# What paces GpSimd's gathers in the first layer: landings of earlier gathers instead of TensorE's progress

## The reference

```python
h = relu(layernorm(x))                                   # 6250 x 128
ef = (relu(edge_attr_64 @ We1 + be1) @ We2 + be2) * sigmoid(edge_weight * Wt + bt)
msg = relu(concat([h[src], ef]) @ Wn1 + bn1) @ Wn2 + bn2
x = x + segment_sum(msg, dst) + h                        # first layer
h = relu(layernorm(x))
h2 = h + segment_sum(h[src], dst)
x = x + relu(relu(h2 @ W1 + b1) @ W2 + b2)               # second layer
```

## Time and profile before

| | us |
|---|---|
| median of three runs | 2865.11 |
| lowest and highest run | 2864.87, 2867.78 |
| span of the profiled execution | 3603.9 |
| GpSimd busy in it | 2098.5 |
| TensorE busy in it | 2652.8 |

### The profile page before, as it was taken

How to read it: one execution, slowest core, us unless ns; L and a number is a source line. 1 busy time by engine, 2 the same in 40 slices (tenths; PEclk the granted TensorE clock), 3 DMA queues, 4 the chain that set the end, 5 groups by cost and what they waited for, 6 DMA issues and landing times.

```text
span 3603.9 us, 51709 instructions
## 1 busy us (share of the span) xinstructions
PE 2652.8 (74%) x14584; PEld 1610.3 (45%) x14585; DVE 1962.6 (54%) x4063; ACT 1009.1 (28%) x1000; POOL 2098.5 (58%) x2125
## 2 busy tenths in 40 slices
PE   4687788877877778778877788785645766766766
PEld 3344444444444444444444444343332545544544
DVE  8665566655656566656655566665673333233333
ACT  3233333333333333333333333232231111111112
POOL 6566666666666666666666665555254555555552
PEclk8788888888888888878888888887875777877777
DMA  6444444444433343444344343333122434334332
GB/s 196 113 127 134 127 127 136 125 130 128 126 121 125 123 124 122 123 125 124 120 122 128 120 128 115 120 117 96 32 101 83 132 118 129 122 95 128 101 114 61
DMA packets 229418, 426.82 MB, mean 118 GB/s; under 512 B 82703, under 2 KB 141584, under 8 KB 229072
## 3 DMA queue, kind: packets, MB, share of 16 engines
q0 software_dynamic: 74752, 153.23, 16.3%
q1 hardware_dynamic: 103152, 177.42, 15.0%
q10 hardware_dynamic: 51266, 93.34, 7.4%
HBM read 364.35 MB, written 59.43 MB: 118 GB/s over the span
## 4 chain that ended last, share of the span: by engine, by line
PE 39%; issue 20%; DVE 17%; another core or an unknown queue 12%; DVEq 10%; SPq 1%; DMA 1%; ACT 0%; POOL 0%; ACTq 0%
PE ps L925 9%; PE ps L836 8%; PE ps L795 8%; DVE nodes L1185 5%; PE ps L804 5%; PE ps L815 4%; PE ps L787 3%; DVEq L1119 3%; DVEq L1165 2%; DVE hot L1140 2%; DVE acc L1127 1%; DVE arena L1185 1%; DVEq L1182 1%; PE ps L915 1%
## 5 line engine op out<-in xcount | busy, mean ns | idle before, releaser
L537 POOL DMA_INDIRECT big<-table,idx x2080 | 2032.9, 977 | 1375.8 <-issue 587.6
L836 PE MATMUL ps<-nodes 128*128 128x500 bf16 x1280 | 448.5, 469 | 335.8 <-DVE nodes L1185 180.3
L795 PE MATMUL ps<-arena,we 128*128 128x512 f32 x784 | 511.9, 784 | 29.7 <-issue 12.2
L640 ACT ACTIVATE big<-big 128x1024 f32<-128x1024 f32 x196 | 207.2, 1057 | 1074.3 <-DVE big L1134 917.5
L815 PE MATMUL ps<-hot,big 128*128 128x64 f32 x3136 | 395.9, 275 | 112.8 <-issue 86.0
L1185 DVE TENSOR_SCALAR nodes<-iota_k,win_off,nodes 128x500 bf16<-128x500 f16 x1280 | 453.7, 407 | 0.0
L815 PEld LDWEIGHTS ps<-hot,big 128*128 128x128 f32 x3136 | 381.6, 195 | 107.0 <-issue 104.6
L1182 DVE TENSOR_TENSOR nodes<-iota_b,nodes 128x384 bf16<-128x384 f16 (+1 forms) x492 | 245.4, 499 | 266.8 <-remote 174.8
L1134 DVE TENSOR_TENSOR big<-ps,big 128x1024 f32<-128x1024 f32 x196 | 239.3, 1221 | 244.2 <-issue 242.6
L836 PEld LDWEIGHTS ps<-nodes 128*128 128x128 bf16 x1280 | 106.3, 106 | 573.6 <-DVE nodes L1185 271.1
L630 ACT ACTIVATE arena<-ps,cols 128x1024 f32<-128x1024 f32 x196 | 218.5, 1115 | 418.7 <-PE ps L787 229.2
(11 more groups left out here) (147 smaller groups left out, 2534.2 us busy)
## 6 DMA issues: line engine op xcount, KB each, us to landing
arena<-in_ew SPq DMA_DIRECT2D x196, 512.0 KB
arena<-in_ea SPq DMA_DIRECT2D x196, 256.0 KB
counts_d<-arena ACTq DMA_DIRECT2D x192, 245.0 KB
acc<-counts_d ACTq DMA_DIRECT2D x15, 2940.0 KB
big<-table,idx POOLq DMA_INDIRECT x2080
table<-big SPq DMA_DIRECT2D x7, 672.0 KB, 3.0
idx<-in_src SPq DMA_DIRECT2D x260, 4.0 KB
xs<-in_x SPq DMA_DIRECT2D x7, 448.0 KB, 5.5
```

Of the source, the lines that this page charges most:

```text
L537: pool.indirect_dma_start(to(u, q, t), None, table, bass.IndirectOffsetOnAxis(ap=idx[:, u, at:at + 1], axis=0))\
L795: pe.matmul(p_ef[q], we2[:, :], hid[:, q, :], start=True, stop=True).then_inc(ef_mm, 1)
L836: m = pe.matmul(to, hots[:, t, :], keys[:, t, :], start=False, stop=True, skip_group_check=True)
```

## The change

The semaphore of a block's gathers becomes two, one for its gathers 0 and 2 and one for 1 and 3. In front of every gather after the first 32, GpSimd now waits for the landing of the gather before the last one. The waits for `ef_mm` and `agg_mm` go, in all bodies. The waits for `pre_made` and for the indices stay. TensorE increments `hid_mm`, `ef_mm` and `pre_mm` once a pair, by two, with its last instruction. SyncE and VectorE wait for four semaphores in place of two. `paced_pair` with `apart=True` belongs to a loop that these inputs don't enter.

```diff
-        gathered = [[sem(f"gathered{u}{q}") for q in (0, 1)] for u in range(RING)]
+        gathered = [[[sem(f"landed{u}{q}{h}") for h in (0, 1)] for q in (0, 1)] for u in range(RING)]
...
                     for q in (0, 1):
-                        sp.wait_ge(gathered[u][q], b * (16 * TB))
+                        for h in (0, 1):
+                            sp.wait_ge(gathered[u][q][h], b * (8 * TB))
...
+            def gather_one(table, to, u, q, t, landed):
+                at = q * TB + t
+                pool.indirect_dma_start(
+                    to(u, q, t), None, table,
+                    bass.IndirectOffsetOnAxis(ap=idx[:, u, at:at + 1], axis=0))\
+                    .then_inc(landed, 16)
...
+            def paced_pair(b, u, apart):
+
+                for q in (0, 1):
+                    for t in range(TB):
+                        if t >= 2:
+                            pool.wait_ge(gathered[u][q][t % 2], b * 32 + 16)
+                        elif q:
+                            pool.wait_ge(gathered[u][0][t % 2], b * 32 + 32)
+                        elif u:
+                            pool.wait_ge(gathered[u - 1][1][t % 2], b * 32 + 32)
+                        else:
+                            pool.wait_ge(gathered[RING - 1][1][t % 2], b * 32)
+                        if apart:
+                            pool.sem_inc(pairs_begun, 1)
+                        gather_one(table0, to_rows, u, q, t, gathered[u][q][t % 2])
...
-            def gather_body(b, free=False):
+            def gather_body(b, apart):
                 for u in range(RING):
                     pool.wait_ge(pre_made, b * (2 * RING) + (2 * u + 2 - 2 * RING))
                     pool.wait_ge(idx_loaded[u], b * 16 + 16)
-                    if not free:
-                        pool.wait_ge(ef_mm, b * (2 * RING) + 2 * u)
                     pool.sem_inc(pairs_begun, 1)
-                    gather_block(table0, to_rows, u, 0, gathered)
-                    if not free:
-                        pool.wait_ge(agg_mm, b * RING + (u - 2))
-                    pool.sem_inc(pairs_begun, 1)
-                    gather_block(table0, to_rows, u, 1, gathered)
+                    paced_pair(b, u, apart)
...
-                    pe.matmul(p_hid[q], we1[k, :], ea_s[k, u, :], start=True, stop=True).then_inc(hid_mm, 1)
+                    i = pe.matmul(p_hid[q], we1[k, :], ea_s[k, u, :], start=True, stop=True)
+                i.then_inc(hid_mm, 2)
...
-                    i.then_inc(pre_mm, 1)
+                i.then_inc(pre_mm, 2)
...
                 for q in (0, 1):
-                    dve.wait_ge(gathered[u][q], (s * NBODY + b) * (16 * TB) + 16 * TB)
+                    for h in (0, 1):
+                        dve.wait_ge(gathered[u][q][h], (s * NBODY + b) * (8 * TB) + 8 * TB)
```

More of the change, by code:

```diff
@@ L532, in _ @@
                 pool.tensor_tensor(x_g, x_g, stages[g % 2], ALU.add).then_inc(xh_made, 1)
+            def gather_one(table, to, u, q, t, landed):
[4 more added lines that the diff above has]
+                    .then_inc(landed, 16)
             def gather_block(table, to, u, q, landed):
                 for t in range(TB):
[L536 to L540, removed]
+                    gather_one(table, to, u, q, t, landed[u][q])
             def gather_pair(table, to, u, landed):
@@ L552, in _ @@
             pool.wait_ge(table0_stored, 16 * NG)
+            def paced_pair(b, u, apart):
[12 more added lines that the diff above has]
+                        gather_one(table0, to_rows, u, q, t, gathered[u][q][t % 2])
             for u in range(RING):
                 pool.wait_ge(idx_loaded[u], 16)
-                gather_pair(table0, to_rows, u, gathered)
-            def gather_body(b, free=False):
+                for q in (0, 1):
+                    for t in range(TB):
+                        gather_one(table0, to_rows, u, q, t, gathered[u][q][t % 2])
+            def gather_body(b, apart):
                 for u in range(RING):
@@ L560, in gather_body @@
                     pool.wait_ge(idx_loaded[u], b * 16 + 16)
-                    if not free:
-                        pool.wait_ge(ef_mm, b * (2 * RING) + 2 * u)
                     pool.sem_inc(pairs_begun, 1)
-                    gather_block(table0, to_rows, u, 0, gathered)
-                    if not free:
-                        pool.wait_ge(agg_mm, b * RING + (u - 2))
-                    pool.sem_inc(pairs_begun, 1)
-                    gather_block(table0, to_rows, u, 1, gathered)
+                    paced_pair(b, u, apart)
             for b in range(1, NBODY):
-                gather_body(b, b >= NBODY - 2)
+                gather_body(b, False)
             pool.wait_ge(sweeps_made, 1)
@@ L575, in _ @@
                 with pool.Fori(NBODY, sweeps * NBODY) as b:
-                    gather_body(b)
+                    gather_body(b, True)
             pool.wait_ge(counts_moved, 16)
@@ L794, in edge_products @@
                         pe.wait_ge(ef_made, n)
-                    pe.matmul(p_ef[q], we2[:, :], hid[:, q, :], start=True, stop=True).then_inc(ef_mm, 1)
+                    i = pe.matmul(p_ef[q], we2[:, :], hid[:, q, :], start=True, stop=True)
+                i.then_inc(ef_mm, 2)
             def message_products(n, m, first):
```

## The result

| | kernel before | changed kernel |
|---|---|---|
| median of the runs, us | 2866.45 (4 runs) | 3408.3 (4 runs) |
| ratio, 95% interval | | 1.1888 (1.1865 to 1.191) |

The change makes the kernel 19% slower, 542 us. The forecast was 3055 us in a range up to 3230: the direction was right, the size was not. The page of the changed kernel: span, busy times, the chain's shares, the two groups that matter, and the gathers' issues with their median time to landing.

What follows compares the result with a forecast made beforehand. The prediction took GpSimd's gathers to leave next to no pause at 10.2 us a pair; landing waits would make it 11.2, adding 192 us over 192 pairs to 2865, other terms 0: 3055 us, range 2765 to 3230.

Steps and rivals of the forecast that it cites:

- The step of a pair in a run: Loop of pairs after the first 32 gathers: 10.2 us a pair in a run, against 12.9 in the profile.
- The floor of 10.0 us: GpSimd in the loop: eight gathers a pair need 10.0 us at the profile's spacing of 1.25 us.
- The pace of the landings: New landing waits on GpSimd: two gathers take 2.80 us, a pair 11.2; 192 us slower, chance 0.43.
- My upper bound: Landing waits on GpSimd at worst: every landing takes 3.0 us, a pair 12.0 us, the kernel 3211 us.
- The stops for TensorE: GpSimd's waits for ef_mm and agg_mm: removing them booked at 0, with a gain of at most 38 us.
- The increments: TensorE sends three increments fewer a pair: booked at 0; the skill's price would give 15 us.
- The rival of starvation: Without stops GpSimd gathers in longer rows and holds TensorE up: 240 us slower, 3105 us, chance 0.15.
- prompt increments: Short gather pauses and fewer increments let TensorE's increments through sooner: 86 us faster, 2779 us, chance 0.32.
- The forecast for the span: Profiled execution of the changed kernel: its span grows by 0 to 100 us over the earlier profile's.
- the prediction's own sign: Profile after: if the span shrinks by more than 100 us, TensorE's increments were the bound.
- The rival of no change: Landings come within 2.2 us, so the waits are over when GpSimd reaches them: 2865 us, chance 0.10.

Runs made afterwards that it cites:

- second profile: The kernel before, unchanged, profiled once more after the result: span 2859.9 us, loop 10.28 us a pair.
- e1_inc_only: The kernel before with one TensorE increment a pair and stage and nothing else: 2862.41 us, ratio 0.9998.
- e3_no_pace: The kernel before without the waits for ef_mm and agg_mm in front of the gathers, none in their place: 2856.27 us, ratio 0.9964.
- e5_one_in_flight: The changed kernel with each gather waiting for the landing of the last gather itself, one in flight: 5461.39 us, ratio 1.9087.

## Why the prediction was right in direction and wrong in size

**The step of a pair in a run**, taken at 10.2 us from the two ratios though the trace said 12.9: right. The second profile shows 10.28, and six gathers show that GpSimd was its bound. This step decided the direction. It assumed that all parts shrink alike, and they nearly did: the loop to 0.80 of its time (2475 to 1974 us), the second layer's gathers to 0.75 (868 to 653). The floor of 10.0 us beside it was too low: it takes the median gather of 0.94 us, while the mean in the earlier trace rows is 1501.28 / 1537 = 0.98, so eight need 10.2 us or a little more and there was no pause left at all. Read from the first profile alone, the paced loop at 11.2 us would have seemed hidden under 12.9.

**The pace of the landings** is the step that failed, as a size. The term is (11.2 - 10.2) x 192 = 192 us; the two profiles show 13.17 - 10.28 = 2.9 us a pair where it had 1.0. In quiet the 2.80 us for two gathers were right: the timeline shows 2.80 (1118.76 to 1121.56), and with no large transfer beside the gathers the median is 2.81. The term had next to nothing for what comes on top. I wrote that gathers beside the loads should land later, and booked 0.04 us for it, four times in a pair. The meetings with large transfers were 276 us of the loss, 1.4 a pair, and half of that is the store of the counts, 245 KB by ScalarE, which didn't occur in the prediction at all. The other part is smaller: without these transfers the loss is 270 us, 0.4 a pair more than the 192 of the sum, by stops whose cause isn't settled.

The sample was of the wrong gathers. It had the last gathers of four pairs, ahead of the loads. In the changed kernel's trace this same distance, from a pair's last gather to the load of indices, has a median of 2.62 us, while a fourth gather, which waits for the second, starts 2.5 us after the third on average. Rows of last gathers can't show what the loads and the store do to the others.

**My upper bound was too low** for the same reason: 3.0 us for two, 12.0 a pair. One row of the trace ahead of the prediction would have warned: a pair whose last gather started at 1005.12 and whose load of indices came 3.8 us later, at 1008.89, stood in the stretch before, and I left it out. A bound has to come from the worst rows, not from the four that stand in a row.

**The stops for TensorE**, booked at 0 with a gain of up to 38 us: right. Their going alone is worth 9 us.

**The increments**, booked at 0: right, within 0.1%. The 26.3 ns for an increment that the Trainium skill gives ("TensorE: Matmul & The Clock Gate", section "The cost: per-tile semaphore tail") would by the prediction's estimate have made 15 us, 0.5%, if all of it were on the path. e1_inc_only excludes that, so they are not on it.

**The rival of starvation** fell with e3_no_pace, and that of **prompt increments** with e1_inc_only (fewer increments gain nothing) and with the second profile (there were no late ones to make prompt). Both rested on the earlier trace rows, that is on one execution; in the second profile and in every variant's these rows have no counterpart. The forecast for the span, 0 to 100 us more, went wrong for this reason: it fell by 195, to the time of a run. By the prediction's own sign, a span shorter by more than 100 us, the increments would have been the bound; that sign compared two executions in different conditions and was worth nothing.

**The rival of no change** was the Trainium skill's figure for a DMA issued by GpSimd ("DMA: Bandwidth & Descriptors", section "Anatomy of one DMA"), 2.15 us for 64 KB. The changed kernel's page has a median of 2.6 us from issue to landing, and one gather at a time needs 2.98 us on average until the next starts. The measurement decides. The 2.98 us hold the meetings with other transfers and the time to start again, which the estimate doesn't; but in quiet too SyncE noticed landings only some 2.6 us after the start.

## What to carry to other kernels

A queue that waits for the landing of the transfer k back goes at k transfers per way, start to landing to next start, including the worst meetings with other transfers: count k so that k issue times exceed nearly every way, not the mean. Here 3 x 1.25 us left 354 stops and a loss of 6%, and 4 x 1.25 us left 47 stops and 18.5 us against no limit at all; single ways of 6.0 us were longer than either. Waits that are over when they are reached cost nothing that shows, so a limit of sufficient depth is nearly free. A tighter one turns hidden latency into the engine's rate, and here two waits of eight, beside the loads, kept 374 us of 542. When a profile is 26% longer than the runs, take a second one before reading mechanisms from it, or read only what the two times together allow.

## What the runs showed of the hardware

- A gather of 128 rows of 512 bytes costs GpSimd 1.25 us (0.94 and 0.30), whether or not it waits for a landing that is already there. The mean over a loop is a little more, 1.28 us (1974 us for 1536 gathers), since some take longer than 0.94.
- One at a time, such a gather takes 2.80 us to the next one's start in quiet and 4.14 beside a load of 768 KB (e5_one_in_flight); with three in flight a single one took 6.0 us.
- TensorE's granted clock, as a share of its full speed, was 0.97 in the window of the loop with six gathers, 0.94 in that of the kernel before (second profile), 0.87 in that of the changed kernel and 0.70 with one gather in flight. In the same windows TensorE was busy for 94, 89, 78 and 48% of the time. The window of the last one:

```profile
104.00:4687.00 4583.00, 2217.68 (x9602) 1483.36 (x9602) 1514.66 (x2933) 814.28 (x769) 1473.18 (x1536) 0.70 0.21 66
```

- In one execution of the kernel before, engines that waited for TensorE's increments started 4.7 to 6.3 us after the end of the instructions that send them, while GpSimd gathered, and the span was 26% longer than a run. No other profiled execution here showed it, and its cause was not found.
